# Macaron block (FFN, attention, FFN): q's store issued ahead of k's reads in batch 0, one batch's FFN and left half in other slots, prologue in another order

## What is computed

```python
x = L0_attn_x                                   # (8, 512, 256), f32
x = x + 0.5 * ffn(layernorm(x))                 # first FFN
x = x + attention(layernorm(x))                 # 16 heads of 8, on the left 128 columns
x = x + 0.5 * ffn(layernorm(x))                 # second FFN

# ffn(x): y = real(ifft(fft(x) @ (w_freq_real + 1j * w_freq_imag))) + bias
# attention(x): left = x[..., :128]; q, k, v = left @ W*.T, 16 heads of 8
#   att = softmax(q k / 4) over the keys; out = (att v) @ Wo.T + bo
```

## Time and profile before

| | us |
|---|---|
| median of 3 runs | 315.89 |
| lowest and highest | 313.49, 320.12 |
| the profiled execution, time | 312.38 |
| the profiled execution, span | 310.5 |
| mean granted TensorE clock | 1.00 of full speed |

### The profile page before, as it was taken

How to read it: one execution, slowest core, us unless ns; L and a number is a source line. 1 busy time by engine, 2 the same in 40 slices (tenths; PEclk the granted TensorE clock), 3 DMA queues, 4 the chain that set the end, 5 groups by cost and what they waited for, 6 DMA issues and landing times.

```text
span 310.5 us, 8810 instructions
## 1 busy us (share of the span) xinstructions
PE 294.8 (95%) x3440; PEld 112.5 (36%) x3443; DVE 190.5 (61%) x552; ACT 257.6 (83%) x285; POOL 98.3 (32%) x113
## 2 busy tenths in 40 slices
PE   8887999899998999999999999999999999998996
PEld 5633333233332333333333333334333333322333
DVE  1688546747775678657776678567755643370255
ACT  2117998898997889998998989998999999999921
POOL 6562531223604053223604251313600340034005
PEclk9999999999999999999999999999999999999999
DMA  7935615573462762665453663554372464112102
GB/s 192 337 137 192 218 65 153 195 270 133 139 217 83 245 208 103 208 204 217 155 192 129 231 205 112 198 172 143 131 238 104 138 205 170 38 68 70 37 34 70
DMA packets 25891, 49.33 MB, mean 159 GB/s; under 512 B 2032, under 2 KB 14192, under 8 KB 24048
## 3 DMA queue, kind: packets, MB, share of 16 engines
q1 hardware_dynamic: 25152, 48.26, 46.0%
q10 hardware_dynamic: 688, 0.40, 0.8%
HBM read 31.08 MB, written 17.56 MB: 157 GB/s over the span
## 4 chain that ended last, share of the span: by engine, by line
PE 75%; DMA 9%; DVE 5%; ACT 5%; issue 3%; POOL 3%; SPq 0%; ACTq 0%; POOLq 0%
PE ot L828 28%; PE misc L719 26%; PE scores L799 15%; ACT probs L669 5%; DMA leftT<-left_scr 4%; DMA q_scr<-qp 2%; PE scores L719 2%; DMA QS<-q_scr 2%; DMA left_scr<-left_blocks 1%; POOL x L553 1%; PE scores L686 1%; PE scores L693 1%; DVE left_blocks L966 1%; DVE lh L957 1%; POOL rstd L550 1%
## 5 line engine op out<-in xcount | busy, mean ns | idle before, releaser
L669 ACT ACTIVATE probs<-scores 128x1024 f32<-128x1024 f32 x256 | 243.8, 1028 | 20.6 <-PE scores L799 20.3
L828 PE MATMUL ot<-probs,VS 128*32 128x512 f32 x1024 | 133.9, 594 | 2.9 <-ACT probs L669 2.3
L799 PE MATMUL scores<-QS,KS 32*128 32x512 f32 x512 | 64.7, 495 | 3.0 <-DMA QS<-q_scr 1.3
L799 PEld LDWEIGHTS scores<-QS,KS 32*128 32x128 f32 x512 | 24.5, 181 | 109.8 <-ACT probs L669 101.0
L828 PEld LDWEIGHTS ot<-probs,VS 128*32 128x32 f32 x1024 | 30.6, 109 | 25.8 <-ACT probs L669 5.0
L563 POOL TENSOR_TENSOR x_out<-x,half_bias 128x512 f32<-128x512 f32 x7 | 9.0, 1292 | 88.8 <-DVE x L1012 88.8
L548 POOL TENSOR_SCALAR veps<-mv 128x4 f32<-128x4 f32 (+1 forms) x25 | 6.1, 242 | 95.9 <-DVE mv L946 95.9
L1017 DVE SCALAR_TENSOR_TENSOR x_out<-misc,rstd,x_out 128x256 f32<-128x256 f32 x28 | 13.5, 484 | 33.7 <-PE misc L719 30.2
L719 PE MATMUL misc<-half_ffn,xT 128*32 128x256 f32 x448 | 32.1, 386 | 0.0
L719 PE MATMUL misc<-half_ffn,xT_in 128*32 128x256 f32 x400 | 27.1, 385 | 1.4 <-DVE half_ffn L1193 1.3
L550 POOL TENSOR_TENSOR rstd<-veps,power 128x4 f32<-128x4 f32 (+1 forms) x25 | 25.3, 1013 | 2.1
(11 more groups left out here) (125 smaller groups left out, 260.0 us busy)
## 6 DMA issues: line engine op xcount, KB each, us to landing
KS<-k_scr SPq DMA_DIRECT2D x14, 512.0 KB, 4.9
QS<-q_scr SPq DMA_DIRECT2D x14, 512.0 KB, 4.6
x_in<-x SPq DMA_DIRECT2D x8, 512.0 KB, 5.1
xT_in<-x_t SPq DMA_DIRECT2D x8, 512.0 KB, 6.4
k_scr<-kp SPq DMA_DIRECT2D x8, 512.0 KB, 3.0
q_scr<-qp SPq DMA_DIRECT2D x8, 512.0 KB, 4.4
x_scr<-x_blocks SPq DMA_DIRECT2D x7, 512.0 KB, 2.9
xT<-x_scr SPq DMA_DIRECT2D x7, 512.0 KB, 4.7
```

The lines of the kernel that those rows point to most:

```text
L669: nc.scalar.activation(probs[u % PRING][:, :, :], scores[u % SRING][:, :, :], ACT.Exp, scale=SCORE_SCALE).then_inc(exp_done, 1)
L799: last = mm(scores[(u + j // 2) % SRING][:, j % 2, :], KS[b % 2][rows, slot, kt * P:(kt + 1) * P].bitcast(F32R), QS[b % 2][rows, slot, :]. ...
L828: last = mm(ot[COL * j:COL * (j + 1), :], VS[b % 2][:, kt, h, :], probs[(u + j // 2) % PRING][:, j % 2, :], start=s % 8 == 0, stop=s % 8 == 7)
```

## The change

It does four things. On SP, q's store of batch 1 is issued ahead of the reads of k's rows. In table FIRST (iteration 1) the jobs F1_1, F1_2, F1_3 of batch 3 go from slots 4, 5, 6 to slots 1, 4, 5. On DVE, iteration 1's left half goes from slots 8 and 9 to 7 and 8. In the prologue ACT makes half_bias two instructions sooner, POOL adds it to batch 0's first two tiles ahead of the first rstd, batch 0's moments and rstd of x1 are computed in two halves, with lh in two halves behind them, and F1_3 of batch 1 is evacuated behind q.

```diff
-FIRST = {**STEADY, 0: [("F1_0a", 2, LEFT), ("F1_0", 2, LEFT)], 1: []}
+FIRST = {**STEADY, 0: [("F1_0a", 2, LEFT), ("F1_0", 2, LEFT)], 1: [("F1_1a", 2, LEFT), ("F1_1", 2, LEFT)],
+         4: [("F1_2a", 2, LEFT), ("F1_2", 2, LEFT)], 5: [("F1_3a", 2, LEFT), ("F1_3", 2, LEFT)], 6: []}
...
             load_x(3)
             k_out(1)
+            q_out(1)
             k_in(1)
-            q_out(1)
             q_in(1)
...
-            rstd_of(0, 1)
             pool.wait_ge(bias_set, 1)
             pool.wait_ge(x_loaded[0], 16)
             add_row(x1[0], x_in[0], half_bias, early_biased, slice(0, 1))
             add_row(x1[0], x_in[0], half_bias, early_biased, slice(1, 2))
+            rstd_of(0, 1)
             add_row(x1[0], x_in[0], half_bias, xb_done, slice(2, T))
             pool.wait_ge(x_loaded[1], 16)
-            add_rows(x1[1], x_in[1], half_bias, xb_done)
-            rstd_of(1, 1)
+            add_row(x1[1], x_in[1], half_bias, ahead_biased, slice(0, 2))
+            pool.wait_ge(first_mv, 1)
+            nc.gpsimd.tensor_scalar(veps[1][:, 0:2], mv[1][:, 0:2, 1], EPS, None, ALU.add).then_inc(first_veps, 1)
+            pool.wait_ge(first_veps, 1)
+            nc.gpsimd.tensor_tensor(rstd[1][0][:, 0:2], veps[1][:, 0:2], power[:, 0:2], ALU.pow).then_inc(first_rstd, 1)
+            rstd_of(1, 1, slice(2, T))
+            add_row(x1[1], x_in[1], half_bias, xb_done, slice(2, T))
...
+            act.wait_ge(bias_loaded, 16)
+            nc.scalar.mul(half_bias[:, :], bias_raw[:, :], 0.5).then_inc(bias_set, 1)
             for piece, bank, copy in ((5, scores[0][:, 0], even[2]), (6, scores[0][:, 1], odd)):
                 act.wait_ge(ffn_mm, piece)
                 nc.scalar.mul(copy[:, :, :], half_bank(bank), 0.5 / E).then_inc(ffn_copied, 1)
 
-            act.wait_ge(bias_loaded, 16)
-            nc.scalar.mul(half_bias[:, :], bias_raw[:, :], 0.5).then_inc(bias_set, 1)
...
                     if it + 2 < B:
-                        if s == (8 if it else 10):
+                        if s == (10 if not it else 7 if it == 1 else 8):
                             left_half(it + 2, range(0, 2))
-                        if s == (9 if it else 10):
+                        if s == (10 if not it else 8 if it == 1 else 9):
                             left_half(it + 2, range(2, T))
```

More of the change, by code:

```diff
@@ L105, in slots_of @@
         ahead = [(f"F1_{t}", 2) for t in range(T)]
-        jobs = [(f"F1_{t}", 1) for t in range(T)] + [("LT", 1)] + ahead + [("KT", 1), ("QT", 1), ("N", 1)]
+        jobs = [(f"F1_{t}", 1) for t in range(T)] + [("LT", 1)] + ahead[:-1] + [("KT", 1), ("QT", 1), ahead[-1], ("N", 1)]
         return {s: [(name, d, LEFT)] for s, (name, d) in enumerate(jobs)}
@@ L321, in build_macaron @@
         rstd_done = [sem(f"rstd_done{i}") for i in range(3)]
+        ahead_biased = sem("ahead_biased")
+        first_stats = sem("first_stats")
+        first_mv = sem("first_mv")
+        first_veps = sem("first_veps")
+        first_rstd = sem("first_rstd")
         normed = sem("normed")
@@ L954, in left_half @@
             def left_half(b, tiles=range(T)):
-                dve.wait_ge(rstd_done[1], b + 1)
+                if b or tiles[-1] == T - 1:
+                    dve.wait_ge(rstd_done[1], b + 1)
                 for t in tiles:
@@ L1204, in _, with first_x1 @@
             fold(half_ffn, even[2], odd[:, :, :], ALU.subtract, ALU.add, 6, 4)
[L1205 to L1208, removed]
+            dve.wait_ge(mv_done[0], 1)
+            norm0_stats(1, range(0, 2))
+            def first_x1(t):
+                dve.wait_ge(evacuated, evac_count(f"F1_{t}", 0))
+                return nc.vector.bn_stats(stats[1][:, t, :], x1[0][:, t, :])
+            evacuate("F1_0", 0)
+            evacuate("F1_1", 0)
+            first_x1(0)
+            evacuate("F1_2", 0)
+            first_x1(1).then_inc(first_stats, 1)
+            dve.wait_ge(first_stats, 1)
+            for t in range(2):
+                last = nc.vector.bn_aggr(mv[1][:, t, :], stats[1][:, t, :])
+            last.then_inc(first_mv, 1)
+            evacuate("F1_3", 0)
+            first_x1(2)
+            first_x1(3).then_inc(stats_done[1], 1)
+            norm_moments(1, 1, range(2, T))
+            dve.wait_ge(first_rstd, 1)
+            left_half(0, range(0, 2))
+            norm0_stats(1, range(2, T))
+            left_half(0, range(2, T))
             norm_moments(0, 2)
-            run_jobs(PROLOGUE, T)
-            for t in range(T):
+            evacuate("LT", 0)
+            for t in range(T - 1):
                 evacuate(f"F1_{t}", 1)
-            run_jobs(PROLOGUE, 2 * T + 1)
-            run_jobs(PROLOGUE, 2 * T + 2)
+            evacuate("KT", 0)
+            evacuate("QT", 0)
+            evacuate(f"F1_{T - 1}", 1)
             dve.wait_ge(row_ready, 1)
             nc.vector.tensor_copy(KS[0][:, 0, :].bitcast(F32R), row_banks[0]).then_inc(first_k_set, 1)
-            run_jobs(PROLOGUE, 2 * T + 3)
+            evacuate("N", 0)
             for n, rows in ((2, KS[0][:, 1, :]), (3, QS[0][:, 1, :])):
```

## The result

The kernel after took 316.44 us at the median of 22 runs (312.31 to 321.06), the kernel before 312.81 us in 22 runs beside them. The ratio is 1.0087, with a 95% interval of 1.0058 to 1.0117: the change makes the kernel about 2.7 us slower. The ratio leaves out the runs more than 1.5% above the fastest of their kernel; the means of all 22 runs lie 3.0 us apart. The loss is within 2%, as forecast, but I had forecast 0.2 us less than before, and a loss of this size lay among the rivals ("leftT late", +2.2) and not in the forecast. That the forecast of 315.7 us stands 0.7 us from the measured median is luck: it was built on a median of three runs of before, 315.89, and 22 runs put that at 312.81. The profiled execution took 317.36 us with a span of 315.6 us, 5.0 us more than the one of before.

A forecast was written before the change was run, and what follows sets the result against it. It took PE, busy 95% of the span, as the bound, so only PE's waits mattered. Terms -1.35 - 0.85 + 2.0 = -0.2 us gave 312.2 us profiled, 315.7 us at the median; range 311.5 to 318.8.

The forecast's parts named there:

- leftT late: Rival, chance 0.12: in iteration 1 q's store takes 6.4 us, leftT lands late (+4.4), sum +2.2 us.
- the further 0.3 us at N: Iteration 1, slot 10: PE idle another 0.3 us at N, beyond near 2.9 us ahead of V_0.
- Behind that the slots keep their lengths: Iteration 1 after N of slot 10: later slots keep their old lengths, so PE reaches KT_0 of batch 3 at 97.2.
- +1.8: Iteration 1: PE reaches KT_0 of batch 3 1.8 us later, the old leftT wait of 1.48 us subtracted.
- +2.0 with the tail: Iteration 1's whole term: +1.8 us at KT_0 plus 0.2 for a tail; bounds -1.48 and +4.4.
- +3.3 with N: Iteration 1, slot 10: PE's N goes at 88.75 in place of 85.42, 3.3 us later.
- So the wait goes whole: -1.35 us: Before batch 1's first scores: storing q ahead of k's reads removes PE's whole 1.35 us wait; other bound 0.
- the prologue's -0.85: Prologue: earlier half_bias and halved statistics bring lh sooner, winning 0.85 us; bounds -0.95 and +1.0.
- four lh of 0.28: Prologue: DVE's queue was added up with four lh of 0.28 us each, the last at about 19.2.
- a lock in the prologue: Rival, chance 0.10: POOL's add and DVE's lh exclude each other, most of the prologue gain lost, sum +0.55 us.
- 0.75 of 0.85: Prologue: the part of the 0.85 us gain lost if lh must wait for POOL's add to end.
- the 0.95 that I had called the most: Prologue: PE's idle time before the transposes, 0.95 us, taken as the largest possible gain.

The follow-up runs named there:

- e2: Kernel before with only iteration 1's part of the change (F1_1 to F1_3 of batch 3 and the left half moved); ratio 1.0132.
- e1: Kernel after with iteration 1's part undone (jobs and left half in old slots), q's store and prologue still changed; ratio 1.0004.
- e9: e3 with POOL also waiting for lh before its overlapping adds, in the prologue and in iteration 1; ratio 0.9963.
- e3: Kernel after with POOL computing batch 3's rstd first in iteration 1, ahead of x2's rstd and begin_x2; ratio 1.0031.
- e11: Kernel after with the left half back in slots 8 and 9 of iteration 1, the FFN jobs still moved; ratio 1.0049.
- e10: Kernel after again, unchanged; ratio to the kernel before 1.0102.
- e4: Kernel after with ten matmuls on zeros filling PE's wait ahead of V_0 in iteration 1; ratio 1.0056.
- e12: The kernel of e4 run again; ratio 1.0084.
- e5: Kernel before with only q's store of batch 1 moved ahead of k's reads; ratio 0.9993.
- e6: Kernel before with only the new prologue; ratio 0.9990.
- e8: e1's kernel with POOL waiting in the prologue for lh before adding onto batch 1's last two tiles; ratio 0.9937.
- e13: Kernel before again, unchanged, in the place of a changed one; ratio 1.0004.
- e14: Kernel before once more, unchanged, in the place of a changed one; ratio 1.0014.
- e7: Kernel before with leftT's read ahead of q's two reads on SP in iterations 1 to 5; ratio 1.0115.
- e15: e8 with leftT's read between q's two reads in iterations 1 to 5; ratio 0.9946.

## Why the prediction was right or wrong

**Right: where batch 1's part loses.** Nearly every station was there: x2's moments late, POOL's rstd of batch 3 last in its queue, DVE idle 2.78 us ahead of lh, V_0 held up by QT_1, no wait for leftT in iteration 1. Only the further 0.3 us at N was not (0.15 in e2, none in after). Counted from DVE's turn of ot in slot 7, rstd was ready after 3.46 us (forecast 3.54) and V_0 went after 4.95 (5.1). e1 and e2 put the whole loss into this part. e9 takes it all away in the trace, and e3 and e11 take away more than half, each at another link.

**Wrong: the step "Behind that the slots keep their lengths".** It took the new wait as idle time only. PE's clock fell in most executions, and in the trace of after the matmuls behind the wait took up to twice their time. This has no term in my sum and costs 0.8 to 1.6 us of the mean, and the trace of before had nothing to read it from: its clock was 1.00 throughout. It is shown by the windows of after and by e10 (same idle time, clock 1.00, 1.31 us less); e4 and e12 show that the falls become rare when the gap is filled.

**Mis-sized: "+1.8".** I subtracted the old wait for leftT, 1.48 us, as if it were always there. In seven traces of kernels with batch 1's old slots (before, e1, e5, e6, e8, e13, e14) that wait in iteration 1 was 1.48, 0, 0, 0, 0.91, 0.64 and 0.42 us: 0.49 on average. The second half of iteration 1 is 16.87 us on average there, and 19.29 with the moved slots at full clock: +2.42, where I had +2.0 with the tail. The stall itself is 2.96 us (19.29 less the 16.33 of e1, which had no wait for leftT), where I had +3.3 with N; the credit was three times too large.

**Mis-sized: "So the wait goes whole: -1.35 us".** It does go whole, but with q's store in its old place it was 1.35, 1.19, 0.50, 0, 0 and 1.01 us in six traces, 0.68 on average. I had taken 0 as the other bound and then the one value seen.

**Mis-sized, and a rival that was right: the prologue's -0.85.** Measured -0.49 (8.12 and 8.11 us against 8.61 and 8.58 from the first FFN matmul to LT). Taking my "four lh of 0.28" as given was the error. The rival "a lock in the prologue" describes what happened: the first lh of the pair lasted until the end of POOL's add. The lock kept 0.6 of a possible 1.1 us, as e8 shows, where I had put 0.75 of 0.85; and with 1.1 e8 passes the 0.95 that I had called the most. And I had thought of that pair only in the prologue: in e3 the same two operations meet in slot 7.

**The sum by what was measured.** -0.68 - 0.49 + 2.42 = +1.25 at full clock, against 1.7 (+-0.5) by the executions. With 0.8 to 1.6 for the clock it is +2.1 to +2.9, against 3.0 between the means of the result's runs and 2.7 by the ratio. Of my error of 2.9 us against the ratio the three terms make 1.45, and the clock most of the rest. All three had been taken more favourably than they are: the prologue's by the lock, and the two waits since the one trace of before held unusually long ones at just the places that the change removes.

**What stays open.** The waits for leftT from iteration 2 on ran from 0.3 to 5.3 us a trace, whatever the kernel (e7 and e15 apart). Whether they are longer on average behind the stall (3.3 us in five traces, against 1.9 in the seven with the old slots) is not settled, and the missing 0.4 us at full clock could be that. Why the clock fell in half of e11's executions is open too, and whether one fall costs the 1.3 us of the trace or the 2.4 us between the executions' means (316.47 less 314.03); executions with a fall may also hold longer waits. No trace here shows the exact cause of the scatter in the DMA landings.

## What to carry to other kernels

A wait of DMA landing that stands in one profile is one draw: before it is credited to a change, read it in several profiles of the same kernel, or give its mean and not its value. When instructions are moved ahead on one engine, walk the queue of the engine that feeds them (here POOL's: rstd, two adds, rstd) and put the urgent result first, or the move only moves the wait ahead of more work. And price a new idle time of PE with the slower matmuls that may follow it: here 2.65 us of it brought 0.8 to 1.6 us more on average, and a wait of 1.89 us was once enough to bring the clock down.

## What the runs showed of the hardware

**PE's clock behind idle time.** In after's trace PE stood 2.65 us without a matmul; the granted clock fell to 0.50 near the end of that and stayed there for some 3.5 us. Behind the same 2.65 and 2.64 us in e2's and e10's traces it was 1.00. By executions it fell in 18 of 28 of after, in 3 of 6 of e2, in 5 of 24 with the gap filled and in 20 of 138 of before. Behind 2.46 us it fell once (e13), behind 1.89 once (e7), and behind 1.91, 2.04, 2.07 and 2.09 it did not (after, e1, e12, e4). So at these lengths it is a matter of chance, and one profile can show either case. The Trainium skill, page "TensorE: Matmul & The Clock Gate", section "What's actually happening", names the two levels and says that idleness of PE leads to the lower one; the three traces with a fall agree, each with PE idle for 1.89 to 2.65 us; the clock fell at the end of that idle time in after, 0.2 us behind it in e7 and 1.1 us behind it in e13.

**GpSimd's add holds up VectorE's scaling.** DVE's scaling of lh (tensor_scalar, f32, SBUF to SBUF, 128 x 128) took 1.54 us for two beside POOL's add of 128 x 512 in the prologue, 1.85 beside two such adds in a row in e3, and 0.56 to 0.60 without them. Each add held one lh, which ended 0.1 us behind the add; POOL's adds kept their 1.27 to 1.29 us. Not every DVE instruction is held: the turn of lh (STREAM_TRANSPOSE, 128 x 512) took 1.19 us beside such an add in e9, and 1.21 without one in before. The Trainium skill, page "SBUF — State Buffer", section "SBUF: two separate sides", says that the one that starts first has the shared ports for the whole instruction; the traces agree in that the add began first (by 0.07 us in the prologue) and lh lasted until its end, and e8 and e9 agree in that the wait goes when the add goes.

**Order on one DMA queue.** leftT's read of 256 KB took 3.5 to 6.8 us behind q's two reads of 512 KB and 2.7 to 2.8 us ahead of them (e7). The same read behind the same neighbours differed by up to 3.3 us within and between traces. The longest waits for it go with the longest reads: 2.46 us in e13 and 2.04 in e1 behind reads of 6.8.
